# Gated cross-attention with a quantised feed-forward: where GpSimd takes the second norm's power in its step

## The chip, the cores and the metric

The kernel runs on one core of one Trainium2 chip. The metric is the device time of the whole kernel in microseconds (us). Three runs of the kernel before are shown, and their median is 336.7 us. One execution was also profiled. "Span" below is the time from its first to its last instruction.

## The reference

The input x has 4 batches of 1024 tokens of 256 values, ctx 4 batches of 77 rows, and a segment number per token (0 to 127).

```python
def reference(x, ctx, seg, g_xattn, g_ffn, Wq, Wkv, Wo, W_in, b_in, W_out, b_out):
    # attention: 16 heads of 16; token t sees rows seg[t] - 0, 1, 2, 3 of k and v
    qh = split_heads(layernorm(x) @ Wq.T)
    k, v = split(ctx @ Wkv.T)
    scores = einsum(qh, k[clip(seg - offsets)]) * 16 ** -0.5   # masked where seg - offset < 0
    out = einsum(softmax(scores), v[clip(seg - offsets)]) @ Wo.T
    x = x + tanh(g_xattn) * out
    # feed-forward of width 1024, on layernorm(x), weights rounded to 8 bits by row or column,
    # activations and hidden values to 16 bits by their largest absolute value over all tokens
    h = gelu(q16(layernorm(x)) @ q8(W_in) + b_in)
    return x + tanh(g_ffn) * (q16(h) @ q8(W_out) + b_out)
def layernorm(x): return (x - mean(x)) / sqrt(var(x) + 1e-5)      # over the last axis
```

## The kernel before, in words

The kernel is written with an explicit instruction order for each engine and semaphores between them. There are 4096 tokens, 32 tiles of 128, which the attention stage takes in 16 pairs u = 0 to 15, two tiles (t = 0, 1) a pair. In that stage, up to about 190 us of the span, a software pipeline runs in steps i. In step i each engine works on several pairs of different age, in a fixed order:

- TensorE (`step`, L804) gathers the keys of a tile of pair i-1 (L746), transposes x of pair i (L794), gathers values, projects queries of pair i (L766), transposes the normalised x of pair i-6 (L783), gathers the second keys, **transposes the attention output o of pair i-3** (`transpose_o`, L737, which waits for GpSimd's o of both tiles), gathers the second values and multiplies pair i-3 by Wo (`attn_out`, L766). Then comes the first gather of keys of the next step.
- VectorE (`step`, L1090) multiplies queries by keys (L1022, out of PSUM) and sums them (L1028) for the two tiles of pair i-1, makes the mask and the maximum (L1034 to L1043), and for pair i-2 the end of the softmax, `probs` (L1058). It adds the attention output to x for pair i-4 (`residual`, L1076), takes statistics of half of the pairs (L992, L1001), forms the norm's bias for pair i-5 (`norm_bias`, L1010 or L1014, which reads GpSimd's `rstd`), and the largest value (L1082). In a few steps (3, 7, 9, 11) it also builds one-hot matrices (L1156), and in step 15 a diagonal and a row of levels of W_out (L1236, L1238).
- ScalarE (`step`, L534) takes the exponential of pair i-2 (L447), evacuates transposes and projections from PSUM (L373, L467), copies values to SBUF for GpSimd (`copy_v`, L443), and evacuates the transposed o of pair i-3 (`evac_oT`). For eight of the pairs (0, 3, 5, 7, 9, 10, 11, 13) it then takes sums and squares (L518, L530). It normalises pair i-5 (L423). The very last item of its step is `var_eps(i-4)` (L506 or L509), which writes `ve`, the variance plus epsilon of pair i-4.
- GpSimd (`step`, L331) weighs the values of pair i-2 with the probabilities. A tile takes three operations: a multiplication (L322), a sum of halves (L325) and a last sum into o (L329). `inv_std2(i-4)` (L307) raises `ve` of pair i-4 to the power -1/2 and writes `rstd` (L313). In steps 4, 7 and 12 it also prepares the first norm's deviation of a batch (L303, L305) ahead of the step.

The first pair weighed by GpSimd is in step 2, and the last one's second tile is done by VectorE (`weigh_last`), so that step 17 has one tile on GpSimd and steps 18 and 19 have only the power. After the pipeline the last outputs are projected, the last norms done, and the feed-forward begins: expansion with Gelu (L919, L621), rounding, contraction (L949). These follow one after the other, as the rounding needs the largest value over all tokens.

Of the kernel before, what the change touches and what calls it, by code (L numbers as in the profile page):

```python
# [32 lines left out]
def flamingo_kernel(nc, x, ctx_kv, seg, g_xattn, g_ffn, w_q, w_kv, w_o, w_in, b_in, w_out, b_out, out):  # L33
# [10 lines left out]
    NP = NT // 2  # L44
# [4 lines left out]
    with ExitStack() as ctx:  # L49
# [201 lines left out]
        def first(u, n):  # L251

            return not isinstance(u, int) or u >= n
# [4 lines left out]
        @block.sync  # L258
        def _(sp):
            sp.dma_start(ctx_ld[0:LKV, :, :], ctx_kv.rearrange("b j d -> j b d")).then_inc(s_ctx, 16)  # L260
            sp.dma_start(wkv_ld[:], w_kv.rearrange("(c p) d -> p c d", p=P)).then_inc(s_wkv, 16)
            sp.dma_start(xres[:, 0:TB // 2, :], x_d[0, :, 0:TB // 2, :]).then_inc(s_xa, 16)
            sp.dma_start(xres[:, TB // 2:TB, :], x_d[0, :, TB // 2:TB, :]).then_inc(s_x[0], 16)
            sp.dma_start(wo_ld[:], w_o.rearrange("(c p) d -> p c d", p=P)).then_inc(s_wo, 16)
            sp.dma_start(win_ld[:], w_in.rearrange("(c p) f -> p c f", p=P)).then_inc(s_win, 16)
            for b in range(1, NB):
                sp.dma_start(xres[:, TB * b:TB * (b + 1), :], x_d[b]).then_inc(s_x[b], 16)
            sp.dma_start(wout_ld[:], w_out.rearrange("(c p) d -> p c d", p=P)).then_inc(s_wout, 16)
            for g in range(NG - 1):
                b, t0 = g * 4 // TB, g * 4 % TB  # L270
                sp.wait_ge(s_x1b, g + 1)
                sp.dma_start(out_d[b, :, t0:t0 + 4, :], xres[:, 4 * g:4 * g + 4, :]).then_inc(s_base, 16)
            sp.wait_ge(s_out, 1)
            sp.dma_start(out_d[NB - 1, :, TB - 4:TB - 2, :], y[(NG - 1) % 2][:, 0:2, :]).then_inc(s_last[0], 16)
            sp.wait_ge(s_base, 16 * (NG - 1))
            for k in range(2):
                sp.wait_ge(s_stored[k], 16 * ((NG - k) // 2))
                sp.wait_ge(s_last[k], 16)


        @block.gpsimd
        def _(pool):
            pool.memset(ident[:], 0.0).then_inc(s_ident0, 1)
            pool.memset(ident16[:], 0.0).then_inc(s_ident0, 1)
            pool.memset(ones[:], 1.0).then_inc(s_const, 1)
            pool.memset(consts[:, 0:TB], LN_EPS).then_inc(s_const, 1)
            pool.memset(consts[:, TB:2 * TB], -0.5).then_inc(s_const, 1)
            pool.wait_ge(s_ident0, 2)
            for m in (ident, ident16):
                pool.affine_select(out=m[:], in_=m[:], compare_op=ALU.not_equal, fill=1.0, base=0,  # L290
                                   pattern=[[-1, P]], channel_multiplier=1).then_inc(s_ident, 1)

            pool.iota(jo[:], pattern=[[1, KW]], base=0, channel_multiplier=1,
                      allow_small_or_imprecise_dtypes=True).then_inc(s_jo, 1)

            def inv_std1(n, at):

                if n < 1:
                    pool.wait_ge(s_mv1, 1)
                    pool.tensor_tensor(ve1[:, at], mv1[:, at, 1], consts[:, 0:TB // 2], ALU.add).then_inc(s_ve1, 1)  # L300
                else:
                    pool.wait_ge(s_ssq1, 4 * n - 2)
                    pool.tensor_scalar(ve1[:, at], ssq1[:, at], 1.0 / D, LN_EPS, ALU.mult, ALU.add).then_inc(s_ve1, 1)  # L303
                pool.wait_ge(s_ve1, n + 1)
                pool.tensor_tensor(rstd1[:, at], ve1[:, at], consts[:, TB:TB + at.stop - at.start], ALU.pow).then_inc(s_rstd1, 1)  # L305

            def inv_std2(u, k):  # L307

                pool.wait_ge(s_ve, u + 1)
                if u >= 2:  # L310
                    pool.wait_ge(s_nb, u - 1)
                    pool.wait_ge(s_xn2, u - 1)
                pool.tensor_tensor(rstd[k][:], ve[k][:], consts[:, TB:TB + 2], ALU.pow).then_inc(s_rstd, 1)  # L313

            def weigh_v(u, k, t):

                n = 2 * u + t
                v = vsel[n % 4]
                v3 = v[:].rearrange("p o (h d) -> p (o h) d", h=H)
                pool.wait_ge(s_vc2, n + 1)  # L320
                pool.wait_ge(s_p, u + 1)
                pool.tensor_tensor(v3, v3, pr[k][:, t].rearrange("p o h -> p (o h)").unsqueeze(2).broadcast_to([P, KW * H, HD]),  # L322
                                   ALU.mult).then_inc(s_pv, 1)
                pool.wait_ge(s_pv, n + 1)
                pool.tensor_tensor(v[:, 0:2, :], v[:, 0:2, :], v[:, 2:4, :], ALU.add).then_inc(s_pv2, 1)  # L325
                pool.wait_ge(s_pv2, n + 1)
                if first(u, 2):
                    pool.wait_ge(s_oTp, u - 1)
                pool.tensor_tensor(o[k][:, t, :], v[:, 0, :], v[:, 1, :], ALU.add).then_inc(s_o, 1)  # L329

            def step(i, k):  # L331
                if 2 <= i < NP + 2:
                    weigh_v(i - 2, k, 0)
                if 2 <= i < NP + 1:
                    weigh_v(i - 2, k, 1)
                if 4 <= i < NP + 4:
                    inv_std2(i - 4, k)

            pool.wait_ge(s_const, 3)
            inv_std1(0, slice(0, TB // 2))  # L340
            inv_std1(1, slice(TB // 2, TB))
            for i in range(2, NP + 4):
                if i in (4, 7, 12):
                    b = (4, 7, 12).index(i) + 1
                    inv_std1(b + 1, slice(b * TB, (b + 1) * TB))
                step(i, i % 2)

            pool.wait_ge(s_bias, 1)
            for g in range(NG):
                v = xres[:, 4 * g:4 * g + 4, :]  # L350
                pool.wait_ge(s_xq, min(g + 3, NG + 1))
                pool.tensor_tensor(v, v, bout[:].unsqueeze(1).broadcast_to([P, 4, D]), ALU.add).then_inc(s_x1b, 1)  # L352

            pool.wait_ge(s_base, 16 * (NG - 1))
            for g in range(NG - 1):
                b, t0 = g * 4 // TB, g * 4 % TB
                pool.wait_ge(s_ys, 4 * g + 4)
                pool.dma_start(out_d[b, :, t0:t0 + 4, :], y[g % 2][:], accum_op=ALU.add).then_inc(s_stored[g % 2], 16)  # L358
# [1061 lines left out]
```

## Time and profile before

| | |
|---|---|
| median of 3 runs | 336.7 us (336.14 to 338.47) |
| profiled execution's own time | 336.22 us |
| its span | 334.4 us |
| mean granted TensorE clock | 0.938 of full speed |
| TensorE matmul busy | 288.5 us (86%) |
| VectorE busy | 293.1 us (88%) |
| ScalarE busy | 254.7 us (76%) |
| GpSimd busy | 167.2 us (50%) |

A busy share is an average over stages with different limits. The chain of waits is followed back from the last instruction, at each step to what released it. Matmuls are pipelined and their listed ends are modelled, so two that follow each other overlap in the list. Spans on GpSimd are rough.

### The profile page before, as it was taken

The numbers are of one execution on the slowest core, as the hardware profiler recorded it, in microseconds if no ns is written. First come the engines' busy times: TensorE is split into PE (matmuls) and PEld (weight loads), VectorE is DVE, ScalarE is ACT, GpSimd is POOL, SyncE is SP. The second block draws the span as 40 slices with busy tenths as digits, with TensorE's granted clock in tenths as the row PEclk, the third lists the DMA queues.
The fourth block names the chain that finished last, engine by engine and source line by source line (L and its number), as shares of the span: only waits on it lengthen the run. The fifth ranks groups of instructions, "written<-read, shape, count | busy, mean of one in ns | idle before, by whom it ended". The sixth has DMA issues, their size and how long they took to land.

```text
span 334.4 us, 6040 instructions
## 1 busy us (share of the span) xinstructions
PE 288.5 (86%) x1847; PEld 213.3 (64%) x1847; DVE 293.1 (88%) x531; ACT 254.7 (76%) x546; POOL 167.2 (50%) x146
## 2 busy tenths in 40 slices
PE   6889986999699899999793938996999859999994
PEld 5666655888578687877672723432444338888883
DVE  1788997999989999999999693799899779999993
ACT  2689956889849787698565575992888969999990
POOL 1107688898798689999959202022234300211111
PEclk9999999999969799999987877996999959999999
DMA  7990000000000000000000001011111100455445
GB/s 224 344 367 4 3 0 0 2 2 2 0 1 2 1 0 2 0 2 2 2 0 1 0 0 66 1 63 63 65 63 63 63 0 1 71 74 99 73 63 125
DMA packets 6742, 15.98 MB, mean 48 GB/s; under 512 B 1270, under 2 KB 3774, under 8 KB 6334
## 3 DMA queue, kind: packets, MB, share of 16 engines
q1 hardware_dynamic: 4303, 11.33, 8.9%
q0 software_dynamic: 1008, 3.67, 7.1%
q10 hardware_dynamic: 1407, 0.69, 0.7%
q8 instruction: 12, 0.20, 0.3%
q14 instruction: 12, 0.10, 0.1%
HBM read 7.82 MB, written 7.86 MB: 47 GB/s over the span
## 4 chain that ended last, share of the span: by engine, by line
PE 47%; DVE 42%; issue 5%; ACT 3%; DMA 1%; DVEq 0%; POOL 0%; ACTq 0%
PE bank L949 17%; PE bank L919 13%; PE bank L766 8%; DVE prod L1022 8%; DVE bank L1028 6%; PE bank L746 5%; DVE onehot L1156 5%; DVE xres L1076 2%; DVE hmax L1316 2%; DVE xmax L1082 2%; DVE w_i L1333 1%; DMA seg_t<-in_itok_BxS_dram 1%; DVE srec L1052 1%; DVE smax L1039 1%; DVE bank L1034 1%
## 5 line engine op out<-in xcount | busy, mean ns | idle before, releaser
L746 PE MATMUL bank<-kvtab,onehot 80*128 80x256 f16 x512 | 68.6, 280 | 4.0 <-DVE prod L1022 3.0
L322 POOL TENSOR_TENSOR vsel<-vsel,pr 128x1024 f32<-128x1024 f32 x31 | 60.2, 1940 | 12.8 <-DVE pr L1058 10.3
L746 PEld LDWEIGHTS bank<-kvtab,onehot 80*128 80x128 bf16 x512 | 51.0, 100 | 16.4 <-DVE prod L1022 4.1
L919 PE MATMUL bank<-xhi,win 128*128 128x512 f16 x128 | 51.3, 401 | 6.5 <-DVE xlo L1311 4.1
L621 ACT ACTIVATE hidden<-bank,bin__58,zscale 128x512 f32 x64 | 47.7, 790 | 11.0 <-PE bank L919 7.5
L919 PE MATMUL bank<-xlo,win 128*128 128x512 f16 x128 | 51.2, 400 | 0.0
L1316 DVE TENSOR_REDUCE hmax<-hidden (+1 forms) x31 | 36.7, 1215 | 10.7 <-ACT hidden L621 10.3
L1376 DVE SCALAR_TENSOR_TENSOR hlo<-hq,rel_wout,hhi 128x512 f16<-128x512 int16 x64 | 45.9, 749 | 0.0
L352 POOL TENSOR_TENSOR xres<-xres,bout 128x1024 f32<-128x1024 f32 x8 | 18.9, 2362 | 49.2 <-DVE xlo L1311 49.2
L1022 DVE TENSOR_TENSOR prod<-bank,q 128x1024 f32<-128x1024 f32 x32 | 39.0, 1218 | 4.2 <-PE bank L746 4.2
L766 PE MATMUL bank<-woT,oT 128*128 128x256 f32 x128 | 35.7, 427 | 6.7 <-DVE xres L1076 3.0
L949 PE MATMUL bank<-wout,hhi 128*128 128x256 f16 x256 | 39.4, 277 | 2.2 <-DVE hhi L1368 2.2
L325 POOL TENSOR_TENSOR vsel<-vsel 128x512 f32<-128x512 f32 x31 | 39.7, 1280 | 2.4
L949 PE MATMUL bank<-wout,hlo 128*128 128x256 f16 x256 | 39.3, 277 | 0.1
L1028 DVE TENSOR_REDUCE bank<-prod 128x64 f32<-128x1024 f32 x32 | 39.0, 1217 | 0.4
L766 PE MATMUL bank<-wqT,xT 128*128 128x256 f32 x128 | 32.5, 398 | 7.2 <-ACT xT L373 6.7
L358 POOL DMA_DIRECT2D out_dram<-y x7 | 6.2, 883 | 59.8 <-ACT y L657 59.8
L638 ACT ACTIVATE hq<-hidden,qh 128x1024 int16 (+2 forms) x32 | 34.5, 1130 | 0.0
L766 PEld LDWEIGHTS bank<-woT,oT 128*128 128x128 f32 x128 | 25.5, 210 | 12.7 <-issue 3.6
L373 ACT ACTIVATE vsel<-bank 128x1024 f32<-128x1024 f32 x31 | 31.3, 1009 | 2.3 <-PE bank L746 2.3
L766 PEld LDWEIGHTS bank<-wqT,xT 128*128 128x128 f32 x128 | 23.4, 193 | 12.7 <-ACT xT L373 9.1
L949 PEld LDWEIGHTS bank<-wout,hhi 128*128 128x128 f16 x256 | 25.4, 100 | 5.8 <-issue 2.5
(152 smaller groups left out, 509.7 us busy)
## 6 DMA issues: line engine op xcount, KB each, us to landing
out_dram<-xres SPq DMA_DIRECT2D x7, 512.0 KB, 2.6
out_dram<-y POOLq DMA_DIRECT2D x7, 512.0 KB, 5.3
xres<-in_x_dram SPq DMA_DIRECT2D x3, 1024.0 KB, 16.0
xres<-in_x_dram SPq DMA_DIRECT2D x2, 512.0 KB, 7.0
win_ld<-in_L_ffn_W_in_dram SPq DMA_DIRECT2D x1, 1024.0 KB, 12.5
wout_ld<-in_L_ffn_W_out_dram SPq DMA_DIRECT2D x1, 1024.0 KB, 20.7
wkv_ld<-in_L_xattn_Wkv_dram SPq DMA_DIRECT2D x1, 512.0 KB, 5.2
ctx_ld<-in_ctx_dram SPq DMA_DIRECT2D x1, 308.0 KB
```

Of the source, the lines that this page charges most:

```text
L322: pool.tensor_tensor(v3, v3, pr[k][:, t].rearrange("p o h -> p (o h)").unsqueeze(2).broadcast_to([P, KW * H, HD]), ALU.mult).then_inc(s_pv, 1)
L325: pool.tensor_tensor(v[:, 0:2, :], v[:, 0:2, :], v[:, 2:4, :], ALU.add).then_inc(s_pv2, 1)
L621: act.activation(hidden[:, g, f, :], bank, ACT.Gelu, bias=bin_[:, f:f + 1], scale=zscale[:, f:f + 1]).then_inc(s_h, 1)
L638: act.activation(hq[m][:, c0:2, :], hidden[:, g, 2 * m + c0:2 * m + 2, :], ACT.Copy, scale=qh[:, 3:4]).then_inc(s_hq, 1)
L746: mm = pe.matmul(dst[:, off * D:(off + 1) * D], onehot[:, off, bass.ds(tile * P, P)], kvtab[:, b, part, col:col + D], start=(part == 0), s ...
L766: mm = pe.matmul(dst[:, t * D:(t + 1) * D], src[:, c, t * P:(t + 1) * P], w[:, c, :], start=(c == 0), stop=(c == C - 1))
L919: mm = pe.matmul(bank, win8[:, c, f * P:(f + 1) * P], part[k][:, c, :], start=(at == 0), stop=(at == 2 * C - 1))
L949: mm = pe.matmul(bank, part[f][:, t * P:(t + 1) * P], wout8[:, f, :], start=(f == 0 and r == 0), stop=(f == FC - 1 and r == 1))
L1022: dve.tensor_tensor(prod[t][:], ps_k[:].rearrange("p (o d) -> p o d", o=KW), q[k][:, t, :].unsqueeze(1).broadcast_to([P, KW, D]), ALU.mult ...
L1028: dve.tensor_reduce(sc[k][:, t].rearrange("p o h -> p (o h)"), prod[t][:].rearrange("p o (h d) -> p (o h) d", h=H), AX.X, ALU.add).then_in ...
L1316: dve.tensor_reduce(hmax[:, bass.ds(g * (FC // 2) + m, 1)], hidden[:, g, 2 * m:2 * m + 2, :], AX.XY, ALU.max, apply_absolute_value=True).t ...
L1376: dve.scalar_tensor_tensor(out=hlo[f][:], in0=hq[f // 2][:, f % 2, :], scalar=rel_wout[:, f:f + 1], in1=hhi[f][:], op0=ALU.mult, op1=ALU.s ...
```

## The change

In each GpSimd step, `inv_std2(i-4)` stands between the two tiles of pair i-2, and no longer behind both. Nothing else is changed: `inv_std2` has the same waits and the same one instruction.

```diff
             def step(i, k):
                 if 2 <= i < NP + 2:
                     weigh_v(i - 2, k, 0)
+                if 4 <= i < NP + 4:
+                    inv_std2(i - 4, k)
                 if 2 <= i < NP + 1:
                     weigh_v(i - 2, k, 1)
-                if 4 <= i < NP + 4:
-                    inv_std2(i - 4, k)
```

## Rows read from the trace of the kernel before

**Rows 1.** Chain that ended last, by engine (the page).
```profile
PE 47%; DVE 42%; issue 5%; ACT 3%; DMA 1%; DVEq 0%; POOL 0%; ACTq 0%
```

**Rows 2.** L313: duration in ns (min/median/max); who waited for it (us, times).
```profile
L313 POOL TENSOR_TENSOR rstd<-ve,consts x16: 695/705/711, 58.9 to 193.1; 128x2 f32<-128x2 f32 x16
...
  DVE nbias L1014: 0.4, 1
```

**Rows 3.** Timeline of GpSimd, steps 13 and 16: start us, duration us, instruction.
```profile
142.03 1.93 POOL L322 TENSOR_TENSOR vsel<-vsel,pr 128x1024 f32<-128x1024 f32 x1
...
146.08 1.93 POOL L322 TENSOR_TENSOR vsel<-vsel,pr 128x1024 f32<-128x1024 f32 x1
...
150.12 0.71 POOL L313 TENSOR_TENSOR rstd<-ve,consts 128x2 f32<-128x2 f32 x1
150.81 1.93 POOL L322 TENSOR_TENSOR vsel<-vsel,pr 128x1024 f32<-128x1024 f32 x1
...
180.16 0.71 POOL L313 TENSOR_TENSOR rstd<-ve,consts 128x2 f32<-128x2 f32 x1
```

**Rows 4.** Timeline of VectorE: the norm bias of step 14.
```profile
152.37 0.32 DVE L1010 TENSOR_SCALAR nbias<-nmean,rstd 128x1 f32<-128x1 f32 x2
```

**Rows 5.** Timeline of ScalarE: variance plus epsilon in steps 4, 9, 11, 16.
```profile
58.49 0.29 ACT L506 ACTIVATE ve<-ssq,consts 128x2 f32<-128x2 f32 x1
...
109.09 0.29 ACT L506 ACTIVATE ve<-ssq,consts 128x2 f32<-128x2 f32 x1
...
129.85 0.30 ACT L506 ACTIVATE ve<-ssq,consts 128x2 f32<-128x2 f32 x1
...
176.13 0.30 ACT L509 ACTIVATE ve<-mv,consts 128x2 f32<-128x2 f32 x1 [0.17 <-DVE mv L1001]
```

**Rows 6.** Timeline of GpSimd: second tile in steps 4 and 11; start of step 12.
```profile
54.88 1.93 POOL L322 TENSOR_TENSOR vsel<-vsel,pr 128x1024 f32<-128x1024 f32 x1
...
126.42 1.93 POOL L322 TENSOR_TENSOR vsel<-vsel,pr 128x1024 f32<-128x1024 f32 x1
...
131.38 0.20 POOL L303 TENSOR_SCALAR ve<-ssq 128x8 f32<-128x8 f32 x1
...
133.26 1.93 POOL L322 TENSOR_TENSOR vsel<-vsel,pr 128x1024 f32<-128x1024 f32 x1
```

**Rows 7.** Timeline of TensorE: transposes of o in steps 5, 10, 11, 12, 16, 17.
```profile
62.22 0.60 PE L737 MATMUL bank<-ident,o 128*128 128x128 f32 x4
...
115.82 0.60 PE L737 MATMUL bank<-ident,o 128*128 128x128 f32 x4
...
124.60 0.63 PE L737 MATMUL bank<-ident,o 128*128 128x128 f32 x4 [0.19 <-ACT xn2T L373]
...
134.09 0.63 PE L737 MATMUL bank<-ident,o 128*128 128x128 f32 x4
...
172.46 0.63 PE L737 MATMUL bank<-ident,o 128*128 128x128 f32 x4 [0.32 <-ACT xn2T L373]
...
180.26 1.12 PE L737 MATMUL bank<-ident,o 128*128 128x128 f32 x4 [3.59 <-POOL o L329]
```

**Rows 8.** Timeline of VectorE: one-hot matrices before the pipeline and in step 9.
```profile
15.48 1.91 DVE L1156 TENSOR_SCALAR onehot<-seg_b,jo,kvp 80x1024 bf16<-80x1024 bf16 x4
...
106.15 3.13 DVE L1156 TENSOR_SCALAR onehot<-seg_b,jo,kvp 80x1024 bf16<-80x1024 bf16 x2
```

**Rows 9.** Timeline of GpSimd beside step 9's one-hot matrices.
```profile
107.66 1.33 POOL L325 TENSOR_TENSOR vsel<-vsel 128x512 f32<-128x512 f32 x1
```

**Rows 10.** Timeline of TensorE: the query projections of steps 10 and 13.
```profile
111.00 2.90 PE L766 MATMUL bank<-wqT,xT 128*128 128x256 f32 x8 [1.67 <-ACT xT L373]
...
139.74 1.99 PE L766 MATMUL bank<-wqT,xT 128*128 128x256 f32 x8 [0.15 <-ACT xT L373]
```

**Rows 11.** Busy time by window: engines PE, PEld, DVE, ACT, POOL, then granted clock.
```profile
112.00:114.00 2.00, 2.00 (x7) 1.54 (x6) 1.93 (x5) 1.86 (x5) 1.08 (x1) 0.50 0.01 4
```

**Rows 12.** Timeline of ScalarE: evacuation of the transposed o of pair 14.
```profile
182.50 0.57 ACT L373 ACTIVATE oT<-bank 128x512 f32<-128x512 f32 x1
```

## The prediction

> **What bounds the kernel now.** I read the page's chain of waits first. It runs over TensorE and VectorE, 47% and 42%, and GpSimd has 0% of it [rows 1]. So nothing that GpSimd does is a bound on average, and the change can only gain where somebody waits for the power. The view of who waits for L313 answers that: of 16 powers one was waited for, by 0.4 us, and that one lies behind the pipeline, where the order on GpSimd stays as it is [rows 2]. Inside the pipeline the power is early. That of step 13 starts at 150.12 and takes 0.71, and the norm bias that reads it starts at 152.37, in VectorE's own order, 1.5 us later [rows 3, 4]. An earlier power has no taker.
>
> Then I read, in the timelines, when the power's input is there. `ve` is the last thing ScalarE writes in its step. In step 4 it is ready at 58.49 + 0.29 = 58.78, while GpSimd has the first tile behind it at 54.88. In step 11 the two are 130.15 and 126.42 [rows 5, 6]. Today the second tile's 4.05 us lies in that gap. The same comparison over the 13 steps from 4 to 16 has the first tile done before `ve` in every one.
>
> **Part by part.** Nothing is added or removed; 13 of the 16 powers move ahead of a tile, those of steps 4 to 16. From step 17 on there is no second tile, and the order is the old one. The moved step issues one instruction and no DMA, and passes no queue but GpSimd's.
>
> 1. *The power itself.* It costs 0.69 from its start to the next multiplication (150.12 to 150.81), now ahead of the second tile instead of behind it. GpSimd's work per step stays 4.05 + 0.69 + 4.03 = 8.77 [rows 3]. Moved alone it costs nothing.
>
> 2. *The new wait.* Behind it on GpSimd stand the second tile's three operations, and behind these the next step. TensorE's transpose of o waits for the second tile, then ScalarE's evacuation, and, as ScalarE works in order, that step's own `ve`. This closes a loop that does not exist today: `ve`, power, second tile, transpose, `ve` of the next step. Its length for a pair whose statistics ScalarE takes: from the transpose to the end of `ve` 124.60 to 130.15 = 5.55 [rows 5, 7]; 0.69 for the power; 4.03 for the tile; 0.10 from the tile's end to the transpose (180.16, where GpSimd starts its next instruction in step 16, to 180.26, where the transpose that waited for it starts [rows 3, 7]); and as much for the hop from `ve` to the power, which no row here shows, an estimate from that hop. Sum 10.47. For the other pairs the way through ScalarE is shorter (3.97 in step 16, 172.46 to 176.43 [rows 5, 7]), and GpSimd's own 8.77 is the floor, with 0.1 where both are about equal.
>
> 3. *Steps 4 to 8.* In step 4 the second tile ends at 58.78 + 0.10 + 0.69 + 4.03 = 63.60, and the transpose that started at 62.22 [rows 7] starts 1.5 late. How much of it reaches VectorE isn't shown by one row; between 0 (it has the gathers ahead of need) and 1.5 I take 1.0, since VectorE comes to its next gathers half a microsecond or so after they are there.
>
> 4. *Steps 9 to 11, a gain.* In step 9 two one-hot instructions take 3.13; four took 1.91 when GpSimd did nothing beside them [rows 8], so two are worth 1.0. The second ends only after GpSimd's sum has ended (107.66 + 1.33 = 108.99, against 109.28) [rows 8, 9]. After the change, GpSimd has nothing to do from about 106.7 until `ve` at 109.38 + 1.0 = 110.4, and VectorE reaches these instructions at 107.1. It gets some 2.1 back. That does not move ScalarE, whose `ve` is at 110.4 anyway, but it takes away what ScalarE waits for next, and the query projection, which had stood idle for 1.67 [rows 10], has less idle time ahead of it. The transpose of step 10 is then set by GpSimd: 110.38 + 0.10 + 0.69 + 4.03 + 0.10 = 115.30, against 115.82: 0.5 early. Step 11's: 8.77 later, 124.07, against 124.60. So the loss of point 3 is gone by here.
>
> The Trainium skill, SBUF, section "Who interferes with whom", says that VectorE's second port pair is GpSimd's, and that it is an exclusive lock. By that rule the whole 2.1 comes back as soon as GpSimd is idle, and the trace's 3.13 against 1.0 agrees.
>
> 5. *Steps 12 to 17, the loss.* Step 12's transpose: 124.07 + 10.47 = 134.5, against 134.09, +0.4. From there the loop leads. Step 12 also has the first norm's deviation, 133.26 - 131.38 and 0.08 ahead of it = 1.96 [rows 6], so 13's transpose comes 8.77 + 1.96 = 10.73 later. Pairs 9, 10, 11 fall in steps 13, 14, 15, so three times 10.47. Step 16 is one of the others: 8.87. Sum 10.73 + 31.41 + 8.87 = 51.0. Before, it was 180.26 - 134.09 = 46.2 [rows 7]. That is +4.8, and with the 0.4 the transpose of step 17 is 5.2 late, at 185.5.
>
> 6. *The tail.* That transpose takes 1.12, so its evacuation can start at 186.7. Before, it started at 182.50, after other work of ScalarE [rows 7, 12]. 1.1 of the lateness is hidden there; 4.2 is left. Everything behind is chained: projection, norms, the largest value, the feed-forward. Nothing there has slack, and its own length doesn't change.
>
> **Sum:** +0.4 up to step 12, +4.8 to step 17, -1.1 in the tail, about +4.2 us. Against the profiled execution's 336.22 that is 340.4. The median of the runs is 0.5 above that execution, which gives 340.9.
>
> **The rivals.**
>
> *A. The clock of TensorE falls in the new waits, slower still.* The granted clock was 0.50, the level of 1.2 GHz, from 112 to 114, behind an idle 1.67 of TensorE, and the projection at 111.00 took 2.90 instead of 1.99 [rows 10, 11]. In the loop TensorE waits 1 to 2 us at the transpose in each step of 13 to 16. At the lower level, the transpose takes 1.12 instead of 0.63 and the projection behind it about 0.9 more, in the loop or next to it: as an estimate about 1 us for each such step, up to four. This gives 342 to 345. For it: stretches at half clock in this stage today stand behind idle times such as the 1.67 and the 3.59 [rows 7, 10]. Against: the pauses at single transposes in the forecast are 1 to 2 us, mostly shorter than these.
>
> *B. The slack hides it, no change to be seen.* Step 12's transpose starts at 134.09, and GpSimd had already come to the next batch's work at 131.38 [rows 6, 7]. If ScalarE's `ve` comes earlier than I think once it is freed of its other waits, the loop is not 10.47 but 9.2 to 10.0. The three loops of point 5 are then 1.4 to 3.8 shorter, and 0.4 to 2.8 of the 4.2 are left: 337.1 to 339.5. For it: point 4 works that way. Against: the row of step 11's `ve` shows no idle time ahead of it [rows 5], so 5.55 is work and not waiting.
>
> *C. The port relief decides, faster.* The place is the one-hot instructions of steps 7, 9 and 11, and the two of step 15. GpSimd, waiting for `ve`, leaves VectorE alone. Prices: 2.1 in step 9; step 11 similarly, about 0.8; up to 1.5 more if step 7 and step 15 fall well. If the loop of point 5 stays within TensorE's slack, VectorE, which is 42% of the chain [rows 1], keeps 1 to 4.4 us of these: 332.3 to 335.7. It decides from the point where the loop is no longer than a step is today; from the transpose of step 12 to that of step 17 that is 46.2 / 5 = 9.2. Against: for that the loop would have to be 1.3 shorter than its rows say. The exclusive lock of the Trainium skill (SBUF, same section) is the mechanism of this rival, too, and by that rule alone the time would be 332.3 to 335.7; the trace shows the price of the lock, but also the loop that outweighs it.
>
> **How the numbers follow.** My forecast (a loss of 2.6 to 5.6 us, its own range 339.3 to 342.3) gets 0.57, A 0.15, B 0.19, C 0.09. The range goes from 337.0, the low end of B, to 344.0, inside A. The unknown of point 3 (0 to 1.5) and that of point 4 (if the clock falls there as today, the 0.5 isn't gained) lie within it. 1% of 336.7, about what a measurement of this kernel can tell from no change, is 3.4 us, so the line is at 340.1. It cuts my own case, seven tenths of which I put above it. Slower by over 1%: 0.7 x 0.57 = 0.40, and A's 0.15, together 0.55. Faster by over 1%: below 333.3, the lower half of C, 0.05. Within 1%: what is left, 0.40.
>
> **What would show it.** On GpSimd a wait for `ve` ahead of the power in some seven of the steps 4 to 16, in the loop steps about 1.5 us each (`ve` 5.55 behind the transpose, against 4.05 for the first tile), and the second tile starting 0.69 behind the power. On TensorE, waits for GpSimd's o at L737 in steps 13 to 17. Distances of these transposes of about 10.5 in steps 13 to 16. One-hot instructions in step 9 of about 1.0 for two. The norm bias doesn't start earlier relative to its neighbours. The feed-forward keeps its length. I am wrong if the transposes of o in steps 12 to 17 keep their 46.2, if the start of step 17's transpose is below 183, or if the tail absorbs more than 1.1.

## The result, and the profile after

The changed kernel takes 342.7 us in the median of 4 runs (342.18 to 343.53), beside 336.64 for the kernel before. The ratio is 1.0172, with a 95% interval of 1.0129 to 1.0216. The forecast was 340.9, from 337.0 to 344.0. The profiled execution took 342.96 us, with a span of 341.2 (before 336.22 and 334.4).

The chain that ended last, by engine, on the page of the changed kernel (before: [rows 1]):

```profile
PE 41%; POOL 25%; DVE 20%; issue 9%; ACT 3%; DMA 1%; POOLq 0%; DVEq 0%; ACTq 0%
```

GpSimd went from 0% to 25%. An engine busy for half of the span is now on the path. The view of L313, the power, says what GpSimd waits for ahead of it (us, times; before: [rows 2]):

```profile
  ACT ve L506: 15.4, 6
  ACT ve L509: 7.4, 3
who waited for it (us, times):
  DVE nbias L1014: 0.4, 1
```

Nobody waits less for the power than before, the same 0.4 us, and GpSimd waits 22.8 us ahead of it (before 8.4). Two of the nine waits lie behind the pipeline, as before. The other seven are in steps 4, 8, 9, 11, 13, 14 and 15; the forecast had "some seven".

The transposes of o on TensorE, steps 5 and 10 to 17 (before: [rows 7]):

```profile
63.65 0.66 PE L737 MATMUL bank<-ident,o 128*128 128x128 f32 x4 [1.30 <-POOL o L329]
...
113.84 0.66 PE L737 MATMUL bank<-ident,o 128*128 128x128 f32 x4 [0.87 <-POOL o L329]
122.67 0.63 PE L737 MATMUL bank<-ident,o 128*128 128x128 f32 x4 [0.19 <-POOL o L329]
133.11 0.66 PE L737 MATMUL bank<-ident,o 128*128 128x128 f32 x4 [0.86 <-POOL o L329]
146.69 0.63 PE L737 MATMUL bank<-ident,o 128*128 128x128 f32 x4
157.14 0.66 PE L737 MATMUL bank<-ident,o 128*128 128x128 f32 x4 [0.86 <-POOL o L329]
167.62 0.65 PE L737 MATMUL bank<-ident,o 128*128 128x128 f32 x4 [0.86 <-POOL o L329]
178.83 0.66 PE L737 MATMUL bank<-ident,o 128*128 128x128 f32 x4 [2.23 <-POOL o L329]
...
187.59 1.12 PE L737 MATMUL bank<-ident,o 128*128 128x128 f32 x4 [3.14 <-POOL o L329]
```

Against [rows 7] they start 1.4 late in step 5, 2.0 *early* in step 10, 1.9 early in step 11, 1.0 early in step 12, and 7.3 late in step 17. The distances from 12 to 17 are 13.58, 10.45, 10.48, 11.21 and 8.76. Four are the forecast ones or near; the first has no wait for GpSimd's o in its row, and is 2.85 longer than forecast. What happened in it, first on GpSimd and then on ScalarE (the changed kernel):

```profile
132.33 0.73 POOL L329 TENSOR_TENSOR o<-vsel 128x256 f32<-128x256 f32 x1
133.14 0.20 POOL L303 TENSOR_SCALAR ve<-ssq 128x8 f32<-128x8 f32 x1
133.42 1.65 POOL L305 TENSOR_TENSOR rstd<-ve,consts 128x8 f32<-128x8 f32 x1
```

```profile
131.42 0.60 ACT L373 ACTIVATE xn2T<-bank 128x512 f32<-128x512 f32 x1 [1.61 <-PE bank L783]
135.18 0.84 ACT L467 ACTIVATE q<-bank,rstd 128x256 f32<-128x256 f32 x2 [3.17 <-POOL rstd L305]
135.91 0.60 ACT L373 ACTIVATE oT<-bank 128x512 f32<-128x512 f32 x1
```

Before, the same two instructions and the product with Wo (`woT`) behind them were these:

```profile
131.66 1.64 POOL L305 TENSOR_TENSOR rstd<-ve,consts 128x8 f32<-128x8 f32 x1
133.84 0.83 ACT L467 ACTIVATE q<-bank,rstd 128x256 f32<-128x256 f32 x2
135.43 1.97 PE L766 MATMUL bank<-woT,oT 128*128 128x256 f32 x8
```

ScalarE's query evacuation (`evac_q`, which waits in L465) of the last batch's first pair reads the first norm's deviation, which GpSimd takes at the start of that very step, behind step 11's delayed second tile. ScalarE stands for 3.17 us with everything behind it, among it the evacuation of o. On TensorE that looks so:

```profile
133.60 1.04 PE L746 MATMUL bank<-kvtab,onehot 80*128 80x256 f16 x8
136.56 3.78 PE L766 MATMUL bank<-woT,oT 128*128 128x256 f32 x8 [1.92 <-ACT oT L373]
140.14 1.91 PE L746 MATMUL bank<-kvtab,onehot 80*128 80x256 f16 x8
```

A pause of 1.92, and the product with Wo at half clock, 3.78 instead of 1.97; the gather behind it takes 1.91 instead of 1.04. The windows give the granted clock (the third figure from the right) as 0.50 here:

```profile
136.00:138.00 2.00, 1.44 (x3) 1.18 (x4) 0.66 (x2) 2.00 (x5) 1.92 (x2) 0.50 0.00 0
138.00:140.00 2.00, 2.00 (x6) 1.50 (x5) 0.20 (x1) 0.75 (x3) 1.92 (x4) 0.50 0.00 0
```

In the same windows VectorE is busy 0.66 and 0.20 of 2.00; its wait of 3.96 that ends at 142.16 is for the gather of keys. Behind the pipeline, ScalarE's evacuation of pair 14 starts at 188.74 instead of 182.50 [rows 12], 6.2 late, and the span ends 6.8 late.

### The profile page after: what moved, and what is told of

Read it like the earlier page. It is cut to its first block, busy times and chain, and to the rows that moved or that the text cites. A ratio compares the mean times of both kernels' runs of the same rounds, so it can differ in the third digit from the quotient of the medians.

```text
span 341.2 us, 6040 instructions
## 1 busy us (share of the span) xinstructions
PE 289.5 (85%) x1847; PEld 213.1 (62%) x1847; DVE 292.0 (86%) x531; ACT 254.4 (75%) x546; POOL 167.2 (49%) x146
## 4 chain that ended last, share of the span: by engine, by line
PE 41%; POOL 25%; DVE 20%; issue 9%; ACT 3%; DMA 1%; POOLq 0%; DVEq 0%; ACTq 0%
PE bank L949 17%; PE bank L919 13%; POOL vsel L322 11%; POOL vsel L325 7%; PE bank L766 4%; POOL o L329 4%; DVE onehot L1156 3%; PE bank L746 3%; DVE prod L1022 2%; POOL rstd L313 2%; DVE hmax L1316 2%; DVE w_i L1333 1%; DMA seg_t<-in_itok_BxS_dram 1%; PE bank L737 1%; DVE bank L1028 1%
## 5 line engine op out<-in xcount | busy, mean ns | idle before, releaser
L746 PE MATMUL bank<-kvtab,onehot 80*128 80x256 f16 x512 | 67.0, 275 | 3.6 <-DVE prod L1022 2.5
L746 PEld LDWEIGHTS bank<-kvtab,onehot 80*128 80x128 bf16 x512 | 49.9, 99 | 15.5 <-DVE prod L1022 3.7
L766 PE MATMUL bank<-woT,oT 128*128 128x256 f32 x128 | 38.3, 451 | 6.5 <-ACT oT L373 2.9
L766 PE MATMUL bank<-wqT,xT 128*128 128x256 f32 x128 | 31.6, 390 | 7.2 <-ACT xT L373 6.8
L766 PEld LDWEIGHTS bank<-woT,oT 128*128 128x128 f32 x128 | 27.1, 223 | 13.4 <-ACT oT L373 5.2
```

The source lines that it names most:

```text
L746: mm = pe.matmul(dst[:, off * D:(off + 1) * D], onehot[:, off, bass.ds(tile * P, P)], kvtab[:, b, part, col:col + D], start=(part == 0), s ...
L766: mm = pe.matmul(dst[:, t * D:(t + 1) * D], src[:, c, t * P:(t + 1) * P], w[:, c, :], start=(c == 0), stop=(c == C - 1))
```

## Experiments

Ratios are to the kernel before, run on the same chip beside it; brackets are 95% intervals. The kernel before had a median of 335.8 to 336.9 us on these chips, so the ratio says more than the time in us. Theory 1 is that two waits cost: the forecast loop through `ve`, and the late deviation of the last batch. In the short diffs, `between` chooses the steps in which the power stands between the tiles. Line numbers of these kernels lie 3 to 6 higher than in the listing.

**E1, the late deviation taken out of the changed kernel.**

```diff
-                if i in (4, 7, 12):
+                if i in (4, 7):
...
                     weigh_v(i - 2, k, 0)
+                if i == 11:
+                    inv_std1(NB, slice((NB - 1) * TB, NB * TB))
                 if 4 <= i < NP + 4:
                     inv_std2(i - 4, k)
```

> The changed order, and the first norm's deviation of the last batch (L303, L305 in the trace of the changed kernel), which ScalarE's query evacuation of step 12 waited 3.17 us for, is taken in step 11 between the two tiles, where GpSimd waits 1.69 us for ve anyway. Theory 1 (two waits: the loop through ve, and this one): the 3.17 us wait is gone, the transpose of o in step 13 comes 8.9 to 9.5 us behind that of step 12 instead of 13.58, and the time is 338.0 to 338.8. Rival (the loop alone; the wait of step 12 is hidden behind it, only GpSimd's own 1.96 us are saved): 340.7.

Measured: 337.51 us, ratio 1.0061 [1.0025, 1.0097]. The query evacuation has no wait (it starts at 132.29, right behind the evacuation ahead of it), and steps 12 and 13 are 134.00 to 142.78 = 8.78 apart instead of 13.58. The other distances are those of the changed kernel: 10.48, 10.46, 11.22, 8.76. The time and this distance are a little below the expected ones. So moving the deviation takes some 1.1% off the changed kernel's 1.7%, and 0.6% is left. The rival's 340.7 is out. (E10 below makes the same move in the old order; the two have to be read together.)

**E2, the late deviation alone, in the old order.**

```diff
                 if 2 <= i < NP + 2:
                     weigh_v(i - 2, k, 0)
+                if i == 12:
+                    inv_std1(NB, slice((NB - 1) * TB, NB * TB))
```

> The order of before, and only that same deviation of the last batch comes 4.05 us later, behind the first tile of step 12 instead of ahead of it. Theory 1: the query evacuation of step 12 waits for it some 3.5 us, TensorE idles and drops to half clock, 339.5 to 341. Rival (that wait is hidden): 336.6.

The batch loop ahead of the step is cut to `(4, 7)`, as in E1.

Measured: 343.24 us, 1.0227 [1.0195, 1.0259], more than expected and at least as much as the whole change. ScalarE and TensorE in step 12:

```profile
138.08 0.84 ACT L472 ACTIVATE q<-bank,rstd 128x256 f32<-128x256 f32 x2 [5.74 <-POOL rstd L305]
```

```profile
139.46 3.78 PE L771 MATMUL bank<-woT,oT 128*128 128x256 f32 x8 [5.46 <-ACT oT L378]
```

I had taken the 4.05 us of a tile less the slack. The wait is 5.74, as GpSimd's step here starts only behind its wait for the probabilities (its first tile at 131.87), which the deviation at the head of the step had not to wait for. Step 13's transpose comes 16.35 behind step 12's, 7.5 more than before, and 7.4 us is the loss.

**E3 and E4, the two halves of the change.** `between` is `4 <= i < 11` in E3 and `12 <= i < NP + 4` in E4.

> The power stands between the tiles only in steps 4 to 10. Theory 1: the part of the change that gains. The transpose of o in step 11 starts at 122.7 (before 124.60), the deviation of the last batch is not late, steps 11 to 17 are those of before: 334.7, 0.6% faster than before. Rival (what VectorE gains in the one-hot instructions is given back, as another engine is the bound afterwards): 336.6.

Measured: 334.67 us, 0.9977 [0.9946, 1.0009]. Not told from the kernel before by this interval. The distances show why it gains less than 1.9 us: from step 12 to 13 it is still 10.11, the evacuation waiting 1.67 for the same deviation.

> The power stands between the tiles only in steps 12 to 16. Theory 1 (the loop by itself, without a late deviation of the last batch): step 13's transpose of o as before, then distances of 10.5, 10.5, 10.5 and 8.8, step 17's at about 183.2 against 180.26, and 338.5, up to 340.5 if TensorE falls to half clock in one more stretch. Rival (position alone costs nothing without the late deviation): 336.6.

Measured: 337.75 us, 1.0066 [1.0022, 1.0109]. The transposes of o start at 142.26, 152.71, 163.19, 174.41 and 183.18 in steps 13 to 17. Those are distances of 10.45, 10.48, 11.22, 8.77: the loop by itself. It costs 0.7%, about 2 us, a little less than expected.

**E5, the first half without the late deviation** (E3's `between` with E1's move).

> As the kernel with the power between the tiles in steps 4 to 10 alone, and the first norm's deviation of the last batch taken between the tiles of step 11. Theory 1: in the former the transposes of o of steps 12 and 13 were still 10.1 us apart (8.86 before), as the query evacuation of step 12 waited for that deviation; that goes away, and the time is 333.5 to 334.3 (0.5 to 0.7% below the kernel before). Rival (the time at the end of the stage is set by VectorE, whatever GpSimd does): 334.7 or more.

Measured: 335.07 us, 0.9957 [0.9930, 0.9985]. Faster than before by 0.4%, somewhat less than the expected 0.5 to 0.7%, which the interval still holds; steps 12 to 13 are 8.78 apart. The time in us falls on the rival's side (334.7 or more), which this run therefore doesn't exclude.

**E6, TensorE's clock kept up in step 12 of the changed kernel.**

```diff
             def attn_out(u, k):
-                pe.wait_ge(s_oT, u + 1)
                 if first(u, 1):
                     pe.wait_ge(s_x1, u)
+                if u == 9:
+                    for r in range(10):
+                        pe.transpose(ps_y[:, r % 4 * P:(r % 4 + 1) * P], ident[:], ident[:])
+                pe.wait_ge(s_oT, u + 1)
```

> The changed order, and TensorE does ten transposes that nobody reads where it idles 1.92 us in step 12, ahead of the product with Wo, so that its clock has less reason to fall. Theory 1 (the late deviation costs some 3 us by itself and about 3 us more through the half clock behind it): the product takes 1.97 instead of 3.78 us, step 13's transpose of o comes 10.5 to 11.5 us behind step 12's instead of 13.58, the time is 339.5 to 341. Rival (the clock's part is hidden behind the wait): 342.5.

Measured: 339.98 us, 1.0082 [1.0043, 1.0122]. The unread transposes fill 1.26 us of the pause, and the product runs at full clock, although it still waits:

```profile
135.26 1.26 PE L778 MATMUL bank<-ident 128*128 128x128 f32 x10
137.34 1.99 PE L769 MATMUL bank<-woT,oT 128*128 128x256 f32 x8 [0.82 <-ACT oT L376]
```

ScalarE's wait for the deviation is unchanged at 3.18, but steps 12 and 13 are 10.79 apart instead of 13.58. So of this distance's excess over E1's 8.78, 4.8 us, 2.8 are the clock and 2.0 the wait, in these executions; the medians agree (0.9% less than the changed kernel, 3 us). The clock's part is not the same each time: in E7 the same pause, 1.91, is followed by a product of 2.84, and the distance is 12.32.

**E7 and E8, by kind of pair.** `between` also asks for `on_act(i - 4)` in E7, and for its contrary in E8.

> The power stands between the tiles only for the pairs whose statistics ScalarE takes (steps 4, 7, 9, 11, 13, 14, 15). Theory 1 (what costs is that ve comes late in these steps, and the deviation of the last batch behind it): all of the loss, 341.5 to 343. Rival (each moved power costs the same, 7 of 13 are moved): 339.5.

Measured: 340.78 us, 1.0142 [1.0094, 1.0190]. That is below the expected time and above the rival's 339.5; by the ratio it is most of the 1.7%.

> The power stands between the tiles only for the pairs whose statistics VectorE takes (steps 5, 6, 8, 10, 12, 16). Theory 1: GpSimd waits at the power about 1 us in step 8 and hardly elsewhere, and no transpose of o waits for it: 336 to 336.8, as before. Rival (each moved power costs the same, 6 of 13 are moved): 339.

Measured: 334.91 us, 0.9954 [0.9915, 0.9992]. The loss is in the seven steps in which ScalarE has sums and squares ahead of `ve`. The other six cost nothing; they gain 0.5%, which I had not expected. "Each moved power costs the same" (339) is out.

**E9 to E12, single moves that were expected not to be late.** E9 moves the power in steps 5, 6, 8 and 10, and the deviation as E1. E10 is the old order with the deviation moved as in E1 and nothing else. E11 moves the power in step 9 alone. E12 is E10 and E11 together.

> The power stands between the tiles in steps 5, 6, 8 and 10 alone (pairs whose statistics VectorE takes), and the deviation of the last batch is taken between the tiles of step 11. Theory 1: no tile waits long for ve, no query evacuation waits for that deviation, step 13's transpose of o comes 8.8 us behind step 12's instead of 10.2 as with all vector pairs moved: 0.7 to 0.9% below the kernel before. Rival (the gain of the vector pairs is noise of TensorE's clock): within 0.3% of the kernel before.

Measured: 334.22 us, 0.9927 [0.9900, 0.9955].

> The order of before; only the deviation of the last batch is taken between the tiles of step 11 instead of at the start of step 12. Theory 1: in the kernel before, the query evacuation of step 12 did not wait for it, so there is nothing to gain: 0 to 0.2% below the kernel before. Rival (that deviation is late by a little in most executions): 0.4% or more below.

Measured: 334.13 us, 0.9889 [0.9856, 0.9923]. A miss: the fastest ratio of all, where I expected nothing. Its evacuation of queries in step 12 indeed didn't wait before. The gain stands elsewhere, on VectorE in step 15 (and in step 11, where two one-hot instructions take 0.99 instead of 2.14):

```profile
160.18 1.85 DVE L1236 TENSOR_SCALAR diag<-ident,top_wout 128x128 f32<-128x128 f32 x1
162.17 1.15 DVE L1238 TENSOR_SCALAR sc_wout<-sc_wout 128x8 f32<-128x8 f32 x1
```

(before) and, in E10,

```profile
160.60 0.29 DVE L1241 TENSOR_SCALAR diag<-ident,top_wout 128x128 f32<-128x128 f32 x1
160.80 0.20 DVE L1242 RECIPROCAL sc_wout<-amax_wout 128x8 f32<-128x8 f32 x1
161.03 1.84 DVE L1243 TENSOR_SCALAR sc_wout<-sc_wout 128x8 f32<-128x8 f32 x1
```

```profile
160.24 0.70 POOL L313 TENSOR_TENSOR rstd<-ve,consts 128x2 f32<-128x2 f32 x1
160.91 1.93 POOL L322 TENSOR_TENSOR vsel<-vsel,pr 128x1024 f32<-128x1024 f32 x1
```

GpSimd is further on, so the diagonal slips in ahead of its multiplication and takes 0.29 (before 1.85), and only the instruction on 8 elements a row waits, 1.84 (before 1.15), until 162.87, just where GpSimd's multiplication ends. The pause of TensorE ahead of step 15's product is 1.07 instead of 1.95, that product runs at full clock, and steps 15 and 16 are 8.71 apart instead of 10.54. The diagonal's luck alone is not enough, though: it takes 0.29 in E5, E9 and E12 too, where the pause is 1.60 to 1.62 and the distance 10.20, 9.26 and 10.20. So where E10's gain comes from is argued from one trace, not shown.

E10 also changes how E1 has to be read. The same move takes 1.1% off the old order, where ScalarE did not wait for the deviation, and 1.1% off the new one, where it did (on different chips). With the deviation early in both, the new order is still 1.0061 against 0.9889, some 1.7% slower. What the trace of E1 shows is that the 4.8 us between steps 12 and 13 are gone and the other distances of steps 13 to 17 stay; how the 1.7% divides between the late deviation and the loop depends on which of the two is taken out first.

> The power stands between the tiles in step 9 alone, where GpSimd then waits some 3.5 us beside the one-hot instructions. Theory 1 (port relief): the two one-hot instructions take 1.1 to 1.4 instead of 3.13 us, ScalarE's exponential of step 10 starts 0.8 us earlier, TensorE's clock does not fall behind its pause of 1.67 us, and the time is 0.3 to 0.6% below the kernel before. Rival (the second tile comes too late in step 9 and takes the gain back): 0 to 0.2% above.

Measured: 335.17 us, 0.9932 [0.9906, 0.9958]. The two one-hot instructions take 0.99 beside GpSimd's wait, TensorE's pause ahead of step 10's query projection is 0.79 instead of 1.67, and the clock is 1.00 from 110 to 120, where it was 0.50 for a time before [rows 11]. But ScalarE now waits 1.69 for the deviation in step 12, and steps 12 and 13 are 11.81 apart instead of 8.86. The rows of the one-hot instructions:

```profile
105.32 0.99 DVE L1159 TENSOR_SCALAR onehot<-seg_b,jo,kvp 80x1024 bf16<-80x1024 bf16 x2
```

> The power stands between the tiles in step 9 alone, and the deviation of the last batch is taken between the tiles of step 11. Theory 1 (two separate gains: the one-hot instructions of step 9 run beside an idle GpSimd, and GpSimd is 1.9 us further on from step 12, so that the diagonal of step 15 misses its multiplication): the gains of the two add, 1.2 to 1.7% below the kernel before. Rival (both remove the same slack, TensorE or VectorE is the bound in between): 0.8 to 1.1%, as the early deviation alone.

Measured: 334.0 us, 0.9945 [0.9916, 0.9973]. A miss of both: theory 1 had 1.2 to 1.7%, the rival 0.8 to 1.1%, and it is 0.6%. The gains don't add. E9 to E12 lie at 334.0 to 335.2 us and don't differ reliably from each other, as E12's chip differs from that of E9 to E11. All of them beat both kernels. E10 has the best ratio and is the smallest edit.

## Why the prediction came out as it did

*No taker for an earlier power* (first part): right, 0.4 us before and after.

*Point 1, the power costs nothing by itself*: right. E8 moves six of them and is not slower.

*Point 2, the loop of 10.47*: right. Distances of 10.45 and 10.48 were measured in the changed kernel, 10.48 and 10.46 in E1, 10.45 and 10.48 in E4. My split was right too: in step 13 of E1 GpSimd waits 1.66 at the power.

*Points 3 and 4, steps 4 to 11*: right as far as the executions can tell. Step 5's transpose was forecast 1.5 late and is 1.4. Step 10's and 11's were forecast 0.5 early and are 2.0 and 1.9. The one-hot instructions of step 9 take 1.40 (forecast 1.0, before 3.13). Part of the larger lead is TensorE's clock, which I had supposed to stay: from 90 to 100 it was granted 0.66 before and 1.00 after, and the transposes of steps 8 and 9 are 10.52 apart (92.87 to 103.39) instead of 11.74. But that is no effect of the order. E2, E4 and E10 have the old order up to there and are 10.50, 10.51 and 10.42 apart. The 1.67 of idle time ahead of step 10's query projection, in the old order 1.67 to 2.33, falls to 0.78; what follows such a pause in the old order goes both ways, here in E2 and in E4:

```profile
110.69 1.99 PE L771 MATMUL bank<-wqT,xT 128*128 128x256 f32 x8 [2.33 <-ACT xT L378]
```

```profile
110.44 3.44 PE L769 MATMUL bank<-wqT,xT 128*128 128x256 f32 x8 [2.33 <-ACT xT L376]
```

From step 5's transpose to step 10's it is 53.60 us before, 51.39, 52.55 and 51.39 in E2, E4 and E10, and 50.19 in the changed kernel. The new order gains 1.2 to 3.4 us in this stretch; the forecast gain was 2.0, from 1.5 late to 0.5 early. Whether it reaches the time is not shown: E3's interval holds 1, and E5, which adds these moves to E10's, is not faster than E10 (0.9957 against 0.9889, on another chip).

*Point 5, steps 12 to 17*: forecast +4.8, measured 54.48 - 46.17 = +8.3. **This is the step that failed**, though the time fell inside the stated range. I counted the first norm's deviation as 1.96 us of GpSimd's own time and stopped there. I did not ask who waits for it once the tile ahead of it is late. GpSimd had finished it with 0.5 us to spare before: L305 ended at 133.30, and the query evacuation started at 133.84. E1, E2 and E6 show what stands in its place: 4.8 us in this one distance, 2.0 as waiting, 2.8 as TensorE's half clock behind it. The excess of 0.74 over the loop's 10.47 between steps 15 and 16 (11.21) is not the clock: E1 and E4 have 11.22 with step 15's product with Wo at full clock (1.96 in E1). That product stands 0.50 for VectorE's residual, which is late there; what makes it late was not tried by itself.

*Point 6, the tail absorbs 1.1*: right, 7.33 late at the transpose, 6.24 at its evacuation. The end is 6.8 late, so what stands behind is 0.6 longer than before; it was forecast unchanged.

*Rival A*: its mechanism came, at a price that I hadn't placed. The dearest pause is the 1.92 of step 12, which the rival did not have. In the loop the clock stayed at 1.00 up to about 168, through pauses of 0.86 in steps 14 and 15; from 170 to 172 it was 0.50, behind the 0.86 and a further 0.50 in step 15:

```profile
169.65 3.57 PE L766 MATMUL bank<-woT,oT 128*128 128x256 f32 x8 [0.50 <-DVE xres L1076]
```

From 180 to 182 it was 0.52, behind the 2.23 of step 16. Neither lengthens the distances (11.21 beside E1's 11.22, where the product took 1.96, and 8.76 in both). *Rival B*: out. *Rival C*: its mechanism is real, as the 0.99 for two one-hot instructions in E11 shows (3.13 before). E5 and E8 to E12 are 0.4 to 1.1% faster than the kernel before, but how much of that is the relief of VectorE is not shown, and in the changed kernel it is outweighed.

So the forecast loss was 4.2 us and the measured one 6.1 in the medians (6.7 in the profiled executions). The median lies in the stated range, 337.0 to 344.0, but 0.4 us above the range of my own case, and inside the numbers that I gave to rival A (342 to 345), whose waits I had put elsewhere. That the total is only 1.8 us low is in part luck: in the pair of profiled executions the loss forecast behind step 12 was 3.5 too small, and 1.4 of that was cancelled by a larger lead at step 11, which is in large part the clock of one execution of the kernel before.

## What to carry to other kernels

When an instruction with a late input moves ahead of work on an in-order queue, list every later instruction of that queue with its readers and their slack, also those that belong to another job. Here the small setup instruction of another norm, with 0.5 us of slack, made the largest single delay, 4.8 us in one step, where the loop that was seen coming cost 1 to 2 us a step. And look at which instruction of one engine falls beside which of the other: moving 1.9 us of GpSimd work one step earlier gained 1.1% by the ratio (0.8% by the medians), though nobody had waited for its result. And before a difference between two profiles is put down to the change, look at the profiles of other kernels that have the same order up to that point: here a gain of 3.4 us in one stretch was 1.2 beside two of them.

## What the runs showed of the hardware

- A VectorE instruction on 8 elements a row took 1.84 us beside a multiplication on GpSimd, and its neighbour on 128 a row 0.29 just ahead of it. Which of the two pays is a matter of 0.3 us. GpSimd pays as well: its last sum, 0.73 us alone, took 0.98 in step 9 of the changed kernel, beside the one-hot instructions. The Trainium skill, SBUF, "Who interferes with whom", calls the shared port pair an exclusive lock; the rows beside multiplications and sums agree. Beside GpSimd's power on 8 elements a row it looks different: in E10 two one-hot instructions took their 0.99 (128.97) and the power 1.76 instead of 1.65.
- One pause of 1.92 us of TensorE cost 2.8 us behind it, and ten transposes that nobody reads, 1.26 us, bought it back (E6).
- The same pause is followed by either clock. Ahead of step 15's product with Wo it was 1.60, 1.61 and 1.62 in E5, E12 and E9, and the product took 3.65, 2.95 and 1.97.
- This also holds ahead of any difference between the kernels: the product with Wo in step 4 took 1.99 us in E1 and E4 and 3.59 in E3's profiled execution, behind the same pause of 1.72. So a single profile of this kernel can be some 2 us off through the clock alone, and runs of one kernel spread by 1%. Ratios over several runs are needed here.
